# Second graph score as four transposed rows spread by transfers, attention half a step later

## What is computed

```python
h = relu(layernorm(x))
# layer 3 (GAT)
h = einsum('bnc,cf->bnf', h, W)
s1, s2 = h @ a1, h @ a2
e = leaky_relu(s1[:, :, None] + s2[:, None, :], 0.2) * adj
att = softmax(e, axis=2)
x = x + elu(att @ h + beta * h)
# layer 4 (GRU), on h = relu(layernorm(x)), three times:
a_ = adj @ h
z = sigmoid(a_ @ W3' + h @ U3' + b3)
r = sigmoid(a_ @ W4' + h @ U3' + b4)
hv = tanh(a_ @ W5' + (r * h) @ U5' + b5)
h = (1 - z) * h + z * hv
x = x + h
```

## Time and profile before

| | |
|---|---|
| median of 3 runs | 1503.29 us (1501.19 to 1504.93) |
| the profiled execution, its own time | 1503.36 us |
| its span | 1501.6 us |
| TensorE busy | 1464.4 us (98%) |
| VectorE busy | 1244.5 us (83%) |
| ScalarE busy | 990.1 us (66%) |
| GpSimd busy | 538.7 us (36%) |
| chain that ended last, by engine | TensorE 91%, VectorE 5%, ScalarE 1%, GpSimd 1%, issue 1% |

### The profile page before, as it was taken

The page is one execution under the profiler, slowest core; times in us unless marked ns, Lnnn a source line. Parts: engine busy times, 40 slices in busy tenths (PEclk is TensorE's granted clock), DMA queues, the critical chain, the costliest instruction groups (busy, mean ns, idle before and its releaser), DMA issues.

```text
span 1501.6 us, 45862 instructions
## 1 busy us (share of the span) xinstructions
PE 1464.4 (98%) x18922; PEld 1237.2 (82%) x18922; DVE 1244.5 (83%) x2517; ACT 990.1 (66%) x1795; POOL 538.7 (36%) x623
## 2 busy tenths in 40 slices
PE   8999999899999997799999999999999999999997
PEld 7898999899888886688888788887887887887886
DVE  4888877989999998888888888888888888888767
ACT  5767767667777776666666666666666666666564
POOL 3876776767888885411101101111111111111000
PEclk9999999999999999899999999999999999999999
DMA  8300000002333234100000000000000000000000
GB/s 267 87 2 0 0 0 2 16 17 45 65 68 65 56 58 59 29 1 1 29 1 2 30 1 1 30 1 1 30 1 1 30 1 1 29 2 1 29 2 28
DMA packets 36839, 40.89 MB, mean 27 GB/s; under 512 B 11872, under 2 KB 31840, under 8 KB 36704
## 3 DMA queue, kind: packets, MB, share of 16 engines
q0 software_dynamic: 4608, 16.78, 5.9%
q1 hardware_dynamic: 32096, 22.10, 4.9%
HBM read 13.71 MB, written 8.39 MB: 15 GB/s over the span
## 4 chain that ended last, share of the span: by engine, by line
PE 91%; DVE 5%; ACT 1%; POOL 1%; issue 1%; DMA 0%; DVEq 0%; POOLq 0%
PE ring L99 43%; PE scores L99 28%; PE scores L1706 3%; PE ring L1506 3%; PE scores L1470 3%; PE ring L1546 2%; PE ring L1775 2%; PE ring L1517 2%; PE ring L1690 1%; PE ring L1847 1%; PE ring L1648 1%; PE ring L1659 1%; PE ring L1671 1%; DVE s L1035 1%; PE ring L1679 0%
## 5 line engine op out<-in xcount | busy, mean ns | idle before, releaser
L543 POOL TENSOR_TENSOR s<-s,mx 128x512 f32<-128x512 f32 x128 | 138.2, 1103 | 56.8 <-DVE mx L1040 56.8
L617 POOL TENSOR_TENSOR r_var_eps<-r_mean_var,eps 128x4 f32<-128x4 f32 x16 | 8.1, 508 | 377.1 <-DVE r_mean_var L1208 377.1
L549 POOL TENSOR_TENSOR s<-s,rtotal 128x512 f32<-128x512 f32 x128 | 130.8, 1059 | 31.6 <-DVE rtotal L1046 31.4
L701 ACT ACTIVATE s<-s 128x512 f32<-128x512 f32 x128 | 77.9, 642 | 69.0 <-POOL s L543 68.8
L1371 DVE TENSOR_TENSOR rhp_lo<-r,rhp_hi 128x1024 fp32r<-128x1024 f32 x47 | 57.6, 1225 | 73.4 <-ACT rhp_hi L916 73.4
L1035 DVE SCALAR_TENSOR_TENSOR s<-scores,mask 128x512 f32<-128x512 f32 x128 | 87.1, 681 | 30.6 <-PE scores L1470 30.6
L881 ACT ACTIVATE r<-r,bias_half 128x512 f32<-128x512 f32 x96 | 64.3, 717 | 58.9 <-DVE r L1342 58.9
L935 ACT ACTIVATE hv<-scores,bias 128x512 f32<-128x512 f32 x94 | 64.7, 689 | 55.0 <-PE scores L99 55.0
L909 ACT ACTIVATE later_w<-ring 128x512 f32<-128x512 f32 x64 | 34.8, 596 | 99.0 <-PE ring L1775 99.0
L713 ACT ACTIVATE pT<-ring 128x512 f32<-128x512 f32 x128 | 66.1, 603 | 42.4 <-PE ring L1506 42.4
L1040 DVE TENSOR_REDUCE mx<-s 128x8 f32<-128x512 f32 x128 | 87.9, 686 | 4.4
(11 more groups left out here) (314 smaller groups left out, 5129.8 us busy)
## 6 DMA issues: line engine op xcount, KB each, us to landing
x<-beta_less_one POOLq DMA_DIRECT2D x16, 512.0 KB, 4.7
x<-o POOLq DMA_DIRECT2D x16, 512.0 KB, 6.6
out_x<-x SPq DMA_DIRECT2D x15, 512.0 KB, 2.9
x<-in_x SPq DMA_DIRECT2D x1, 6144.0 KB, 25.4
later_w<-in_L_gnn_w_w SPq DMA_DIRECT2D x3, 512.0 KB, 6.4
x<-in_x SPq DMA_DIRECT2D x2, 512.0 KB, 5.3
x<-in_x SPq DMA_DIRECT2D x1, 1024.0 KB, 7.4
stage<-in_L_gnn_w_qkv SPq DMA_DIRECT2D x3, 256.0 KB, 3.1
```

The lines of the kernel that those rows point to most:

```text
L543: pool.tensor_tensor(sr, sr, mx[:, r, :].unsqueeze(2).to_broadcast([P, CT * 2, N]), ALU.subtract).then_inc(s_shifted, 1)
L549: pool.tensor_tensor(sr, sr, rtotal[:, r, :].unsqueeze(2).to_broadcast([P, CT * 2, N]), ALU.mult).then_inc(p_ready, 1)
L701: act.activation(s[:, par, r, :, :, :], s[:, par, r, :, :, :], ACT.Exp).then_inc(p_exp, 1)
```

## The change

The diff is long; in words, for the halves:

1. **s2.** For the 14 chunks from the third on (`graph_a` of groups 0 to 6), the 8 matmuls of `graph_s2` go. In their place one transpose (L1908 of the new file) turns the s2 column of the four tiles into 4 rows of 128, into ring bank 3; it stands between the two halves (m = 0, 1) of w5. ScalarE copies the rows to SBUF (`s2_rows`), the SP queue writes them to DRAM (2 KB) and, when that has landed, reads them back by two transfers that repeat each row over the 64 partitions of a graph, into `e`. VectorE then adds s1 to `e` in one operation of 128 partitions (`graph_scores_spread`) in place of two of 64.
2. **Attention half a step later.** The scores' sum, leaky relu, mask and maximum move from the end of halves 1 and 3 to halves 2 and 4 (`graph_s`), after `agg_low`; `graph_attention` moves from before `agg_low` to after `r_sum` of the same half; `graph_attT` from before w4 to the end of the half, after w5; `copy_attT` from between the updates to the head of halves 3 and 5 (now `graph_b`), right after r*h; `graph_aggregate` from after w4 to halves 3 and 5, between `adjacency` and u5; `graph_out` with it.
3. **Leaving state.** The transposes of the finished state go to ring banks 0 and 1, after w5, and `leave` goes to the next half, after r*h.
4. **Order within a half.** w4 comes before the first two graph products, the last two products after w3 (into banks 0 and 1, which need `r_added`); ScalarE makes the high part of r*h before it copies `tok`, and the copies of u3 alternate with the tanh of z; all four copies of the products stand at the end of its half; `r_tanh` before them. `norm_rows` of the odd chunk goes from half 5 to half 0.

```diff
+                def spread_s2(c):
+
+                    sp.wait_ge(s2_rows_copied, c - 1)
+                    sp.dma_start(s2_dram, s2_rows[:]).then_inc(s2_out, 16)
+                    sp.wait_ge(s2_out, 16 * (c - 1))
+                    for g in range(2):
+                        own = slice(g * N, (g + 1) * N)
+                        sp.dma_start(e[own, :, :], s2_dram[:, own].unsqueeze(0).to_broadcast([N, CT, N]))\
+                            .then_inc(s2_spread, 16)
...
+                def graph_scores_spread(c):
+                    dve.wait_ge(hw_copied, (c + 1) * FT)
+                    dve.wait_ge(s2_spread, 32 * (c - 1))
+                    dve.tensor_tensor(e[:], e[:], hw[:, :, D:D + 1].to_broadcast([P, CT, N]), ALU.add).then_inc(e_sum, 1)
+                    graph_rectified(c)
...
                     dve.scalar_tensor_tensor(r[:], r[:], 1.0, s.h_before()[:], ALU.add, ALU.mult).then_inc(rh_done, 1)
+                    if s.left is not None:
+                        leave(s.left, ring, 0)
+                    if s.graph_b is not None:
+                        copy_attT(s.graph_b, ring, 3)
                     dve.wait_ge(rh_hi_ready, n)
                     dve.tensor_tensor(rhp.lo[:], r[:], f32(rhp.hi[:]), ALU.subtract).then_inc(rh_lo_ready, 1)
...
                         for m in range(FT):
+                            if m == 1 and s.graph_s is not None:
+                                pe.wait_ge(s2_rows_copied, s.graph_s - 1)
+                            if m == 1 and s.graph_b is not None:
+                                pe.wait_ge(attT_copied, s.graph_b + 1)
                             product(pe, ring[:, 2 + m, :], columns(wT["u3"], m), moving(hp[s.me])).then_inc(hu_ready, 1)
...
+                        if m == 0 and s.graph_a is not None:
+                            wait_apart(pe, hw_copied, (s.graph_a + 1) * FT)
+                            pe.transpose(ring[0:CT, 3, 0:P], hw[:, :, D + 1], ident[:]).then_inc(s2_rows_ready, 1)
+                    if s.graph_s is not None:
+                        pe.wait_ge(hu_copied, n * FT)
+                        graph_attT(s.graph_s, ring, 3)
```

More of the change, by code:

```diff
@@ L1278, in enter, with leave @@
                                           ALU.subtract).then_inc(h0_lo_ready, 1)
-                def leave(c, psum=ring, bank=2):
+                def leave(c, psum, bank):
                     for q in range(2):
@@ L1729, in begin, with final_rows @@
                         product(pe, high[:, 2 + m, :], columns(wT["w5"], m), moving(agg), ends=False)
-                    pe.wait_ge(hu_copied, FT)
+                    pe.wait_ge(first_hu_copied, FT)
                     enter(1, 1)
+                def final_rows(s, bank):
+                    for q in range(2):
+                        for t in (2 * q, 2 * q + 1):
+                            for f in range(FT):
+                                at = (t % 2) * D + f * P
+                                last = pe.transpose(ring[:, bank + q, at:at + P],
+                                                    h[s.other][:, f, t * P:(t + 1) * P], ident[:])
+                        last.then_inc(final_ready, 1)
                 def close_w5(s):
@@ L1813, in half @@
                         pe.wait_ge(g_hT_lo_ready, (s.graph_a + 1) * FT)
+                        if s.graph_b is not None:
+                            pe.wait_ge(x_plus_pos, (s.graph_b + 1) * 2)
                         graph_product(s.graph_a, 0)
                         graph_product(s.graph_a, 1)
[L1816 to L1823 removed]
@@ L1824, in half @@
-                    if s.graph_a is not None:
-                        pe.wait_ge(hw_copied, s.graph_a * FT + 1)
-                        graph_product(s.graph_a, 2)
-                        graph_product(s.graph_a, 3)
-                    if s.graph_b is not None:
-                        graph_aggregate(s.graph_b)
-                    if not s.last:
-                        for m in range(FT):
-                            product(pe, high[:, m, :], columns(wT["w3"], m), moving(agg)).then_inc(z_ready, 1)
@@ L1833, in half @@
-                    if s.graph_a is not None:
-                        graph_s2(s.graph_a)
+                    for m in range(FT):
+                        product(pe, high[:, m, :], columns(wT["w3"], m), moving(agg)).then_inc(z_ready, 1)
+                    if s.graph_a is not None:
+                        pe.wait_ge(r_added, (n + 1) * FT)
+                        graph_product(s.graph_a, 2, ring, 0)
+                        graph_product(s.graph_a, 3, ring, 0)
+                    if s.closing:
+                        pe.wait_ge(h_done, n * FT)
+                        pe.wait_ge(hu_copied, n * FT)
+                        final_rows(s, 2)
+                        close_w5(s)
+                        return
@@ new lines, in half @@
+                    pe.wait_ge(hv_done, n * FT)
+                    for m in range(FT):
+                        product(pe, high[:, 2 + m, :], columns(wT["w5"], m), moving(agg), ends=False)
+                        if m == 0 and s.graph_a is not None:
+                            wait_apart(pe, hw_copied, (s.graph_a + 1) * FT)
+                            pe.transpose(ring[0:CT, 3, 0:P], hw[:, :, D + 1], ident[:]).then_inc(s2_rows_ready, 1)
+                    if s.graph_s is not None:
+                        pe.wait_ge(hu_copied, n * FT)
+                        graph_attT(s.graph_s, ring, 3)
@@ L1850, in half @@
-                    if s.closing:
-                        close_w5(s)
-                    else:
-                        pe.wait_ge(hv_done, n * FT)
-                        for m in range(FT):
-                            product(pe, high[:, 2 + m, :], columns(wT["w5"], m), moving(agg), ends=False)
+                        pe.wait_ge(r_added, (n + 1) * FT)
+                        final_rows(s, 0)
                 keep_clock(high[:, 0, :], 48)
@@ L1921, in build @@
                       beta=a["L1_gnn_ln_beta"])
-        network(nc, x, ident, (scores, ring), (first, second), a, out)
+        network(nc, x, ident, (scores, ring), (first, second), a, out, s2_dram)
 INPUTS = ["x", "adj", "L0_gnn_Wq", "L0_gnn_bq", "L0_gnn_Wk", "L0_gnn_bk", "L0_gnn_Wv", "L0_gnn_bv",
```

204 lines of the change are left out of this document (111 added, 93 removed).

## The result

The changed kernel takes 1515.12 us, the median of 4 runs (1513.30 to 1515.46), against 1503.24 us of the kernel before beside it (1501.19 to 1504.93): a ratio of 1.0075, with an interval of 1.0062 to 1.0087, 11.9 us slower. I had forecast 1502.2 us and no change, with a range that ended at 1514. The profiled execution took 1515.01 us.

What follows compares the result with a forecast made beforehand. TensorE, issuing back to back, was taken to bound the second stage. Savings of 12.3 us against costs of 9.0, 0.35 and 1.75 gave -1.2 from 1503.36: 1502.2 us, no change; range 1491 to 1514, own range 1496 to 1509.

Steps and rivals of the forecast that it cites:

- TensorE's saving: Second stage: second score saves 0.68 us, moved aggregation 0.20; 0.88 a chunk over 14 chunks, 12.3 us.
- The 4-column transpose: Replaces the second score's matmuls within w5: priced at 0.12 us, with bounds of 0.11 and 0.31.
- a tile of its own: If the 4-column transpose counted as a separate tile, the gain would be 0.67 us a chunk, 9.4 us in all.
- So the copy is 0.64 us late: VectorE's transposed-attention copy holds up u3's second bank in halves 3 and 5: 14 waits, 9.0 us.
- 0.4 us either way: Error allowed on the late copy's timing, part of the prediction's own range of 1496 to 1509 us.
- 2.5 us for its own loop branches: TensorE's waits for its loop branches from 800 to 1500 us in the kernel before; no term in the sum.
- Half 0: VectorE begins 0.5 us late, `leave` precedes r*h's low part, u5 waits: 0.25 us a group, 1.75 over 7.
- The 0.35 us for the copies of `tok` in half 5: ScalarE copies `tok` behind the late r*h's high part, and adjacency needs it: 0.35 us over 7 groups.
- The copy isn't late: Rival: VectorE's chain is 0.6 us shorter, only savings remain: 1491 us, or 1494 with half 0's term; chance 0.30.
- The spread rows land late: Rival: s2 rows' transfers exceed 7.5 us, VectorE stops before the updates, 14 us a microsecond, up to 1544; chance 0.12.
- VectorE's lateness spreads: Rival: r_sum also late before half 3's last two products, 0.5 to 1 us, 7 times: 1508 to 1512; chance 0.18.
- the mild case of late rows: Spread s2 rows only 0.5 to 1 us late in reaching VectorE: 1509 to 1516 us.

Runs made afterwards that it cites:

- e1: Changed kernel with z's sum of halves 2 and 4 moved behind the copy of the transposed attention, into the next half: 1497.08 us, ratio 0.996 to the kernel before.
- e3: Changed kernel with GpSimd's softmax shift on one column of 64 from the third chunk on: 1510.02 us, ratio 1.004 to the kernel before.
- e2: Changed kernel with 12 more warm-up transposes at TensorE's start (60 for 48): 1508.49 us, ratio 1.0033 to the kernel before.
- e6: The kernel before with 12 more warm-up transposes at TensorE's start: 1502.97 us, ratio 0.9999 to the unedited one.
- e10: e4 with `leave` moved behind the low part of r*h in half 0: 1499.55 us, ratio 0.9974 to the kernel before.
- e4: Changed kernel with z's sum behind the copy and 12 more warm-up transposes together: 1492.40 us, ratio 0.9926 to the kernel before.
- e8: Changed kernel with the s2 rows written to DRAM six times, each write waited for: 1551.71 us, ratio 1.0323 to the kernel before.
- e9: e4 with the old 8 matmuls of the second score put back ahead of the transpose, result unread: 1502.21 us, ratio 0.9993 to the kernel before.
- e7: Changed kernel with the s2 rows written to DRAM three times, each write waited for: 1514.27 us, ratio 1.0067 to the kernel before.
- e11: Changed kernel with ScalarE making the high part of `agg` before z's second tanh in halves 2 and 4: 1513.77 us, ratio 1.0069 to the kernel before.

## Why the prediction was wrong, by its own steps

**TensorE's saving was right.** Forecast 12.3 us, 0.88 a chunk. From the first u3 of one group to that of the next pass 111.90 us before (963.10 to 1075.00) and 113.83 after (967.85 to 1081.68), 1.93 more. The losses in that group are 2.34 (two stops for the copy), 1.13 (u3's block at the loop is 4.03 and not 2.90), 0.07 (the loop's first stop at the end of the stretch is 0.76, and was 0.69) and 0.22 in half 0 (adjacency 1.23 for 1.09, u5 2.98 for 2.90), 3.76 together; so 1.83 was saved, 0.92 a chunk or 12.9 us over the 14, taking this group for all. The largest part is the second score: 0.80 less the transpose's 0.11 is 0.69, where I had 0.68. The 4-column transpose, which I priced at 0.12 between 0.11 and 0.31, costs 0.11: no way in and out of small tiles is paid, and the trace gives its tile as 128*4. The smaller gain that a tile of its own would have left is out. (I had put it at 0.67 a chunk and 9.4 us; by my own terms, 0.80 - 0.31 + 0.20, it is 0.69 and 9.7.) The Trainium skill's page TensorEngine Tiling (Array Packing), Restrictions, says that column tiling disables transpose mode for FP32 input; the trace agrees, with 0.11 us.

**The step that failed: "So the copy is 0.64 us late".** Place, count, cause and sign were right, and the term of the sum was mis-sized: 9.0 us forecast, 16.4 measured. By the blocks of u3, 4.19 and 4.13 us where e1 has 3.00 and 2.98, a stop costs 1.17 us, and there are 14. Its parts, from the end of adjacency at 993.08 to TensorE's start at 1008.08:

| | forecast | measured |
|---|---|---|
| `agg_low` | 1.87 | 1.88 |
| scores | 1.72 | 1.70 |
| both updates | 4.11 | 4.40 |
| r_sum | 1.20 | 1.20 |
| attention | 1.54 | 1.54 |
| low part of h, z_sum | 2.40 | 2.41 |
| r*h, copy, semaphore | 1.88 | 1.87 |
| VectorE in all | 14.72 | 15.00 |
| TensorE to u3's second bank | 14.08 | 13.95 |
| late | 0.64 | 1.05 |
| and the stop itself | 0 | 0.12 |

Seven tenths of the miss in lateness, 0.29 of 0.41 us, are in one row: the updates beside GpSimd, which e3 takes back. I had read them in half 1, where GpSimd works beside them too, but on operations of 128x4 elements, and L1324 (L1362 in the changed kernel) takes 0.72 us:

```profile
972.42 0.72 DVE L1324 SCALAR_TENSOR_TENSOR hv<-later_w,hv 128x512 f32<-128x512 f32 x1
972.68 1.33 POOL L621 TENSOR_TENSOR g_rstd<-g_var_eps,minus_half 128x4 f32<-128x4 f32 x1
```

The change moved GpSimd's operation of 128x256 elements onto the updates, and I didn't ask what it does to its new neighbour. The trace before had a hint: the same operation takes 1.52 us there, beside r*h of 128x1024 elements (982.62, L628), and 0.99 in its new place. The rest, 0.13, is TensorE: u5 takes 2.83 us of that stretch and not 2.99, and tok 0.79 and not 0.87, while the first bank of u3 takes 1.49 and not 1.39. The 0.12 for restarting I hadn't priced at all. Since the two lists are 14 and 15 us long and the result is their difference, 2% of either is half of the term; I had named 0.4 us either way, which is 5.6 us over 14, and the truth was at that edge, plus the restart.

**The step that was missing: the stops at the loop.** "2.5 us for its own loop branches" was read and left as a constant, so the sum has no term for it. It isn't one: the second stop costs 4 times 1.1 to 1.4 us, and e2 took 6.6 us off in all. e2 and e6 together show that the cost depends on what stands ahead of the loop in TensorE's stream, and not on the added instructions themselves. Why, no run here shows.

**Half 0: a right size with a reason half wrong.** Forecast 0.25 us a group because VectorE begins half 0 0.5 us late and `leave` stands ahead of the low part; measured 0.22 in blocks, 1.5 us in all. The lateness was right: r*h starts at 1063.92, 0.56 us behind u3. But e10 shows that `leave` isn't the cause of the rest: the low part waits for ScalarE's high part, which by luck takes as long. The 0.35 us for the copies of `tok` in half 5 don't show: adjacency takes 0.98 us there as in half 3.

**The sum.** -12.9 + 16.4 + 5.3 (1.13 once and 1.4 three times, by the blocks of u3) + 1.5 is +10.3 of the 11.9 us. Of the other 1.6, about 0.6 lie at the entrance of the stage. From u3 of its opening half (606.24) to the `graph_rows` of half 1 (632.23) pass 25.99 us, and before 25.40: TensorE had stood still for 2.96 and 1.60 us just ahead of it (before: 2.95 and 1.62), the granted clock from 604 to 609 us is 0.53 (before 0.50), which is the 1.2 GHz level, and the matmuls follow each other by 0.43 us. From 609 to 612 us the granted clock is 0.64 here and was 0.84 before: the full rate came back later. Another 0.3 are the loop's first stops (2.8 us together, before 2.5). The rest stays open. e4 gains 1.9 us less than e1 and e2 apart; 1.5 of that are again the first stops, 2.8 us in e4 as in the changed kernel, 1.9 in e1 and 2.2 in e2.

**The rivals.** *The copy isn't late* was wrong here, but e4 shows what it would have given: 1492.4 us, where I had worked out 1491 to 1494. *The spread rows land late*: they are there 4.5 us after the end of ScalarE's copy (987.26), under my 5.2 to 7.3, and 3.1 us before they are wanted; its price of 14 us a microsecond was right (e8, 2.67 us late, +36.6). *VectorE's lateness spreads*: no wait for r in front of the graph products is in the profile. The time came out 3 us above its range of 1508 to 1512, and in a way that no rival described: one known term that was larger, and a constant that wasn't one. It lies within the 1509 to 1516 of the mild case of late rows too, whose mechanism isn't there: that the range of a rival holds the time says nothing for the rival.

## What to carry to other kernels

When an operation is moved past a wait, write both engines' lists between the common event and the meeting point, and distrust a small difference: here 0.64 us between lists of 14 and 15 us came out at 1.05; then look whether one item of the late list may stand behind the meeting point. Here one pass of 1.2 us did, and turned 12 us lost into 6 us won (e1), or 11 with the stops at the loop gone as well (e4).

Look what each moved operation runs beside in its new place: VectorE's rate in one half isn't its rate in another where GpSimd works on larger operands. And when a kernel's loop shows waits for issue, time it again with a few harmless instructions ahead of the loop before a change of some 5 us is judged.

## What the runs showed of the hardware

- TensorE's stops at a loop's ends can depend on what stands ahead of the loop: the same loop stops once at each of 4 ends, 0.24 to 0.93 us (the kernel before, e2, e4, e6, e9, e10), or twice, the second time for 0.83 to 1.45 us after seven matmuls (the changed kernel, e1, e3, e7, e8, e11). Twelve transposes ahead of it take the second stop away (e2), and change nothing where there was none (e6).
- A fp32 operation of VectorE on 128x512 elements with two inputs in SBUF takes 0.69 us, and 0.99 beside a GpSimd operation of 0.99 us on 128x256 elements in SBUF; with GpSimd's on 128x4 elements it takes 0.69 again (e3).
- A stop of TensorE costs about 0.1 us more than the time that its first matmul comes late (0.12 in the mean at the copy): the next matmul issues 0.33 us after it and not 0.23.
- A transpose with a stationary operand of 4 columns costs 0.11 us of issue, like one of 128.
- A 2 KB write from SBUF to DRAM and the wait for its landing take 1.16 to 1.19 us on the SP queue; a read that repeats it over 64 partitions (64 KB) lands in 2.7 us.
